# Softmax sums on 64 partitions by columns of ones beside V, reciprocals in pieces, single K and V buffers

## The reference

```python
Q = (x @ Wq + bq) * scale ; K = (x @ Wk + bk) * scale ; V = x @ Wv + bv
Qr = transpose(Q.reshape(B*H, 64, L)) ; Kr = K.reshape(B*H, 64, L)
w = softmax(Qr @ Kr)                       # 8192 x 8192 for each of 32 heads
x = layernorm(x + (w @ Vr).reshape(B, L, D) @ Wo + bo)
gamma = mean(abs(W)) ; Wq1 = clip(round(W1 / (gamma + 1e-5)), -1, 1)   # W2 alike
x = layernorm(x + relu(x @ Wq1.T + b1) @ Wq2.T + b2)
```

## Time and profile before

| | |
|---|---|
| median of 3 runs | 2467.16 us (2321.94 to 2620.44) |
| profiled execution | 2328.56 us |
| its span, slowest core (6) | 2326.9 us; cores 2295.7 to 2326.9 |
| granted TensorE clock | 0.972 on core 6, 0.972 to 0.978 over the cores |
| TensorE busy | 2127.2 us, 91% |
| ScalarE busy | 1936.2 us, 83% |
| VectorE busy | 605.4 us, 26% |
| GpSimd busy | 185.1 us, 8% |

### The profile page before, as it was taken

One profiled execution on the slowest core, in us unless ns is written; L12 is line 12 of the kernel. 1 busy time (PEld: TensorE's weight loads), 2 busy tenths in 40 slices (PEclk: granted clock), 3 DMA queues, 4 the chain that ended last, 5 costly groups with the idle time before them and its releaser, 6 DMA issues.

```text
span 2326.9 us, 48854 instructions; the slowest of 8 cores (2295.7 to 2326.9 us)
## 1 busy us (share of the span) xinstructions
PE 2127.2 (91%) x17698; PEld 1108.4 (48%) x17712; DVE 605.4 (26%) x796; ACT 1936.2 (83%) x2050; POOL 185.1 (8%) x253
## 2 busy tenths in 40 slices
PE   2999859999988999999999999999999999999498
PEld 0455435455444455555454555555455555554143
DVE  0334223344446441111122111011131111011332
ACT  0589759899988899999999999999999999999000
POOL 0000020000012000001111000010120000011200
PEclk8999879999999999999999999999999999999799
DMA  9556454556656541224302111243211112343147
GB/s 171 124 138 140 106 150 124 116 151 168 164 163 183 169 137 52 74 92 137 114 18 80 47 56 56 92 133 96 73 29 56 47 51 69 101 131 112 29 155 256
DMA packets 95811, 253.33 MB, mean 109 GB/s; under 512 B 29792, under 2 KB 30048, under 8 KB 94048
## 3 DMA queue, kind: packets, MB, share of 16 engines
q1 hardware_dynamic: 86496, 220.45, 32.3%
q0 software_dynamic: 9088, 29.76, 5.9%
HBM read 224.71 MB, written 33.85 MB: 111 GB/s over the span
## 4 chain that ended last, share of the span: by engine, by line
PE 60%; ACT 13%; DMA 12%; issue 6%; DVE 5%; another core or an unknown queue 2%; POOL 1%; ACTq 0%; DVEq 0%; SPq 0%; POOLq 0%
PE psO L749 25%; PE psF L652 16%; ACT PT L782 13%; PE psS L722 10%; PE psS L697 4%; PE psS L724 4%; DMA rec_bc<-rec 3%; DMA den<-den 2%; PE psF L697 2%; DMA rec<-rec 1%; DMA Wch<-W 1%; DMA x<-x 1%; DMA den<-o_sb 1%; DVE A L933 1%
## 5 line engine op out<-in xcount | busy, mean ns | idle before, releaser
L782 ACT ACTIVATE PT<-psS 128x1024 bf16<-128x1024 f32 x2048 | 1934.8, 1034 | 214.3 <-PE psS L724 198.3
L749 PE MATMUL psO<-PT,V 64*65 64x512 bf16 x8192 | 1328.9, 378 | 0.6 <-ACT PT L782 0.2
L722 PE MATMUL psS<-Q,K 64*128 64x512 bf16 x2048 | 770.9, 376 | 38.2 <-ACT PT L782 15.1
L724 PE MATMUL psS<-Q,K 64*128 64x512 bf16 x2048 | 779.3, 381 | 0.0
L749 PEld LDWEIGHTS psO<-PT,V 64*65 64x65 bf16 x8192 | 560.8, 108 | 339.9 <-issue 119.7
L722 PEld LDWEIGHTS psS<-Q,K 64*128 64x128 bf16 x2048 | 190.8, 93 | 439.0 <-issue 381.4
L652 PE MATMUL psF<-x1T,ring 64*128 64x512 bf16 x1536 | 311.6, 379 | 12.5 <-DVE hT L834 11.7
L652 PE MATMUL psF<-ring,hT 64*128 64x512 bf16 x1536 | 280.8, 377 | 4.0 <-DVE x L841 2.8
L724 PEld LDWEIGHTS psS<-Q,K 64*128 64x128 bf16 x2048 | 190.6, 93 | 34.3 <-issue 3.2
L834 DVE TENSOR_SCALAR hT<-psF,b1c 128x512 bf16<-128x512 f32 x106 | 74.7, 747 | 334.5 <-PE psF L652 324.1
L933 DVE TENSOR_TENSOR A<-o_sb,rec_bc 64x512 bf16<-64x512 f32 x64 | 66.4, 1037 | 281.6 <-DMA rec_bc<-rec 280.6
(11 more groups left out here) (74 smaller groups left out, 769.9 us busy)
## 6 DMA issues: line engine op xcount, KB each, us to landing
ring<-wq SPq DMA_DIRECT2D x192, 512.0 KB, 3.8
Wch<-W SPq DMA_DIRECT2D x128, 512.0 KB, 5.1
wq<-qout SPq DMA_DIRECT2D x64, 256.0 KB, 5.6
Q<-qs SPq DMA_DIRECT2D x64, 128.0 KB, 4.6
rec_bc<-rec POOLq DMA_DIRECT2D x32, 256.0 KB, 4.0
x<-x POOLq DMA_DIRECT2D x16, 512.0 KB, 8.6
y<-x SPq DMA_DIRECT2D x16, 512.0 KB, 2.9
xT<-xT POOLq DMA_DIRECT2D x4, 1024.0 KB, 36.3
```

Of the source, the lines that this page charges most:

```text
L722: e.matmul(psS[:, at:at + 512], K[h % 2][0:64, g * 128:g * 128 + 128], Q[0:64, q:q + 512], start=True, stop=True, tile_position=(0, 0))
L724: e.matmul(psS[:, at + 512:at + 1024], K[h % 2][64:128, g * 128:g * 128 + 128], Q[64:128, q:q + 512], start=True, stop=True, tile_position ...
L749: return e.matmul(psO[0:65, half * 512:half * 512 + 512], V[h % 2][lo:lo + 64, v:v + 65], PT[lo:lo + 64, at:at + 512], start=(g == 0 and s ...
L782: e.activation(PT[:, (s % PTR) * 1024:(s % PTR) * 1024 + 1024], psS[:, (s % 2) * 1024:(s % 2) * 1024 + 1024], AF.Exp, scale=SOFT_SCALE).th ...
```

## The change

- V's tile gets 128 columns, 64 of V and 64 of ones, so rows 64 to 127 of `psO` all hold the sums. `o_sb` is 128x1024. `denominators`, `reciprocals`, their four DMAs, `den` and `rec_bc` go.
- `invert` becomes eight reciprocals of 64x128 from `o_sb`'s rows 64 to 127 into `rec`, `divide` two halves as before. `side_plan()` gives these ten items and the preparation's chunks each a step of its own that is not next to an eviction.
- The preparation goes on every fourth step where that is free (before: fourth, and sixth for the quantised ones), with longer gaps around the block's start, and has three `Wch` buffers. W1's last chunk is at step 568, W2's at 785; the first f1 group is at 602, the first f2 at 806.
- One K and one V. All of heads 1 to 3 go through `stg` and DRAM and are loaded in quarters during the last block of the head before, each when its quarter has been used. V's quarter is two DMAs of 128x8 rows of 128 bytes.
- `O_AT` is 25. An o group waits for the two blocks that it reads.
- The loads of bo and b2 stand behind the first scores, on their own semaphore, which GpSimd waits for.

VectorE's list around the start of the second block, before: copies of `psO`, evictions of K of head 1, chunks (`gcol<-Wch`), and the sums' items.

```diff
-REC_AT, MUL_AT, O_AT = 11, 19, 21
+CR = 3 ; O_AT = 25 ; RECS = 8 ; KV_AT = 22
+def side_plan():
+    ...
+    def is_free(s, long):
+        return not (s in norm or s in ends or s - 1 in ends or s + 1 in ends or long and s + 2 in ends
+                    or s % STEPS in (1, 2, 3) or long and s % STEPS == 0)
+
+    for p in range(NB * NP - 1):
+        s = STEPS * (p + 1) + 4
+        for k in range(RECS + 2):
+            while not is_free(s, False):
+                s += 1
+            norm[s] = (p, k)
+            s += 1
+    s = 6
+    for i in range(128):
+        if i in (32, 64):
+            s += 14
+        while not is_free(s, i >= 64) or i >= 64 and s + 1 in norm:
+            s += 1
+        prep[s] = i
+        s += 4
...
-STAGED = [g for g in PRO + ATT if g[0] == "q" or (g[0] == "k" and g[1] >= 2)]
+STAGED = [g for g in PRO + ATT if g[0] == "q" or (g[0] in "kv" and g[1] >= 1)]
...
-    o_sb = alloc("o_sb", [65, 1024], F32)
-    rec_bc = alloc("rec_bc", [64, 1024], F32)
+    o_sb = alloc("o_sb", [128, 1024], F32)
+    rec = alloc("rec", [64, 1024], F32)
...
+            def load_kv(h, m):
+                p = NP * h - 1
...
+                e.wait_ge(pS, STEPS * p + 16 * m + 16)
+                e.dma_start(K[:, m * 1024:m * 1024 + 1024],
+                            AP(ksh, h * 524288 + m * 1024, [[4096, 128], [1, 1024]])).then_inc(sK[m], 16)
+                e.wait_ge(pV, value_count(p, 8 * m + 7))
+                for j in (2 * m, 2 * m + 1):
+                    e.dma_start(AP(V, j * 1024, [[8192, 128], [128, 8], [1, 64]]),
+                                AP(vsh, h * 524288 + j * 64, [[4096, 128], [512, 8], [1, 64]])).then_inc(sV[m], 16)
...
-                if kind == "o" and i == 0:
-                    e.wait_ge(sW["o"], 16)
-                    e.wait_ge(vMul, 2 * NP * (h + 1))
+                if kind == "o":
+                    if i == 0:
+                        e.wait_ge(sW["o"], 16)
+                    e.wait_ge(vMul, 2 * (NP * h + 2 * i + 2))
...
+                if p % NP == 0 and h >= 1 and r % 16 == 0:
+                    e.wait_ge(sK[r // 16], 16 * h)
...
+                if p % NP == 0 and h >= 1 and fb == 0:
+                    e.wait_ge(sV[m], 32 * h)
...
-                    return e.matmul(psO[0:65, half * 512:half * 512 + 512], V[h % 2][lo:lo + 64, v:v + 65],
+                    return e.matmul(psO[:, half * 512:half * 512 + 512], V[lo:lo + 64, v:v + 128],
...
+            e.memset(AP(V, 64, [[8192, 128], [128, 64], [1, 64]]), 1.0)
...
+            def invert(p, k):
+                if k == 0:
+                    e.wait_ge(vO, p + 1)
+                c = k * (1024 // RECS)
+                e.reciprocal(rec[:, c:c + 1024 // RECS], o_sb[64:128, c:c + 1024 // RECS]).then_inc(vRec, 1)
...
-            e.wait_ge(sBias, 6 * 16)
+            e.wait_ge(sBias, 4 * 16)
...
+                if s in NORM:
+                    normalize_queries(*NORM[s])
```

More of the change, by code:

```diff
@@ L24 @@
 WR = 6
+CR = 3
+O_AT = 25
 SOFT_SCALE = float(2.0 ** -10)
@@ L128, in bank @@
     return i % 3, (G - 3 if i >= 3 else G - 1 if i == 0 else -1)
[L132 to L136, removed]
+def side_plan():
+    ends = set(ENDS)
+    norm, prep = {}, {}
+    def is_free(s, long):
[9 more added lines that the diff above has]
+    s = 6
     for i in range(128):
         if i in (32, 64):
-            s += 12
-        while s in busy or s % STEPS in (1, 2, 3, 4, REC_AT, MUL_AT):
+            s += 14
+        while not is_free(s, i >= 64) or i >= 64 and s + 1 in norm:
             s += 1
[L142 to L153, removed]
+        prep[s] = i
+        s += 4
+    return norm, prep
+NORM, PREP = side_plan()
+NORMED = {p: s for s, (p, k) in NORM.items() if k == RECS + 1}
+assert all(NORMED[NP * h - 1] < HSTEPS * h + O_AT for h in range(1, NB))
+THR_AT = {s: i // 32 for s, i in PREP.items() if i in (31, 63)}
 QUANT_END = [next(s for s, i in PREP.items() if i == n) for n in (95, 127)]
@@ L185 @@
 SR = 3
+KV_AT = 22
 def build_nc():
@@ L520, in _ @@
             e.wait_ge(pS, 1)
-            prep_load(0)
-            prep_load(1)
+            e.dma_start(bo_bc[:, :], AP(boh, 0, [[0, 128], [1, 1024]])).then_inc(sBias2, 16)
+            e.dma_start(b2_bc[:, :], AP(b2h, 0, [[0, 128], [1, 1024]])).then_inc(sBias2, 16)
+            for i in range(CR):
+                prep_load(i)
             chunk = 0
@@ L746, in one @@
                     lo = 64 * upper
-                    v = (fb * 8 + 2 * m + odd) * 65
+                    v = ((2 * m + odd) * 8 + fb) * 128
                     at = ((2 * g + half) % PTR) * 1024 + odd * 512
-                    return e.matmul(psO[0:65, half * 512:half * 512 + 512], V[h % 2][lo:lo + 64, v:v + 65],
-                                    PT[lo:lo + 64, at:at + 512], start=(g == 0 and side == 0 and odd == 0),
+                    return e.matmul(psO[:, half * 512:half * 512 + 512],
+                                    V[lo:lo + 64, v:v + 128], PT[lo:lo + 64, at:at + 512], start=(g == 0 and side == 0 and odd == 0),
                                     stop=(g == 31 and side == 1 and odd == 1), tile_position=(lo, 0))
@@ L796, in _ @@
             e.memset(warm[0:1, 0:8], 0.0).then_inc(vInit, 1)
-            for i in range(2):
-                e.memset(AP(V[i], 64, [[4160, 128], [65, 64], [1, 1]]), 1.0)
-            e.memset(vstg[:, :], 1.0)
+            e.memset(AP(V, 64, [[8192, 128], [128, 64], [1, 64]]), 1.0)
             def evacuate(G):
@@ L948, in _ @@
                     take_sums(p)
-                if r == REC_AT and p >= 0:
-                    invert(p)
-                if r == MUL_AT and p >= 0:
-                    divide(p)
+                if s in NORM:
+                    normalize_queries(*NORM[s])
                 if s in PREP:
@@ L960, in _ @@
             take_sums(p)
-            invert(p)
-            divide(p)
+            for k in range(RECS + 2):
+                normalize_queries(p, k)
             for G in range(NATT, len(GROUPS)):
```

166 lines of the change are left out of this document (59 added, 107 removed).

## The result

The changed kernel takes 0.975 of the time before, 95% interval 0.971 to 0.979: 2262.56 us against 2320.18 us, the lowest of four runs each.

A forecast was written before the change was run, and what follows sets the result against it. ScalarE and TensorE were taken as full at 0.965 us a step, with some 94 us lost in attention stalls. 2328.6 - 62.5 (trip) - 14 (prologue) - 10.7 (tail) + 5 (burst) + 5 (preparation, reciprocals) = 2251.4 us; range 2215 to 2305.

The forecast's parts named there:

- the burst: Stretch at 317 us: Wo and four tiles of x still load at once there, so 5 us of its loss was left.
- how the numbers follow: Closing odds: within 2225 to 2282 us 0.70; faster by over 2% 0.75, within 2% 0.16, slower 0.09.
- a lower clock: Rival: 64 more columns of ones lower TensorE's granted clock; gain gone at 0.96, 2471 us at 0.9; chance 0.06.
- the term of the preparation: W1 and W2 chunks at four-step spacing: store waits mostly hidden, 5 us allowed together with the reciprocals.
- The trip, -62.5 us: Attention: removing the sums' four DMAs through DRAM, and the waits for them, was to save 62.5 us.
- six stretches: Disturbed stretches at 242, 317, 660, 742, 800 and 1490 us, laid to the sums' trip, losing 62.5 us together.
- Reciprocals: VectorE, each query block: eight 64x128 pieces of 850 ns plus divides take 8.9 us, fitting ten steps of 9.65 us.
- 128 columns: 0: Value matmuls: weight loads 15 ns shorter if anything, beside matmuls, so 0 us; bounds 0 and 40 us gain.
- K and V: Single buffers loaded by quarters: V's at most 17.8 us a quarter, landing before need, so 0 us.
- Prologue and tail: Start: first exponential at 70.6 us, -14 us; end: output groups run during the reciprocals, -10.7 us.
- Crowding by reciprocals: Rival: VectorE's longer reciprocals delay an eviction each block; 1.2 us pieces give 2318 us; chance 0.09 no change, 0.03 slower.
- The wait only changes its DMA: Rival: VectorE still waits for chunk loads and stores, half of the 62.5 us returns, 2283 us; chance 0.07.

## Why the prediction was right or wrong

**The number.** 2251 us was made for executions like the profiled one; those take 2262.56 and 2263.92 us, 11 and 13 more, and the direction and the 2% were right. In the attention the forecast left 18.5 us in the stretches (8.5 for the preparation, 5 for the burst, 5 for stores and reciprocals) and 34.2 are there; 4.6 us less are lost outside of them, which I had not counted, and that part is luck. The median of all four runs, 2344.91, lies outside 2215 to 2305. The step that failed there is how the numbers follow: I gave a lower clock 0.06 and held it for something that the change might bring, though two of the three runs shown of before lay 6% and 13% above the lowest. A range for the median had to reach up by as much. Of the mechanism, the step that failed is the term of the preparation, below.

**The trip, -62.5 us.** Right in kind: no such wait is left. Mis-sized: alone it is 51.6 us in the attention. I took the whole of six stretches for it, and behind it stood waits for chunks and for the threshold that it had hidden. The 5 us that I left for the burst are about half of the 11 us that are missing.

**The preparation, 5 us together with the reciprocals.** This step failed most. The stretches of the preparation went from 8.5 to 34.2 us. I had worked out that a store buffer comes back after 8.2 us against 7.7 us for eight steps, and took the difference for some tenths of a us that the room between evictions would hide. Two things were wrong. The 8.2 us were built on the median landing of 5.6 us: in front of the stall at 604 us the stores took 8.62, 6.99 and 7.22 us to land, and a buffer came back after 8.2 to 11.9 us, 10 on average. And the lateness doesn't end with each pair of chunks: it adds up over a row of them (7.5 us over eight, the rows above), until the next eviction or copy of sums pays for it. In all VectorE waited 68.1 us for stores, and ScalarE stood for 8.21, 3.90 and 6.92 us at 604, 653 and 710 us. Four buffers take 20 us off. The forecast set the chunks' six-step spacing against four steps and did not ask what six steps had hidden. The threshold I left as it was; its 24 us against 11 steps show as soon as VectorE is not late for another reason, and are worth 8 us.

**Reciprocals.** 153 + 128 x 5.4 = 850 ns; measured 903 ns, 830 in a row (6.63 / 8):

```profile
L732 PEld LDWEIGHTS psO<-PT,V 64*128 64x128 bf16 x8192 | 499.9, 94 | 379.3 <-issue 138.1
...
L903 DVE RECIPROCAL rec<-o_sb 64x128 f32<-64x128 f32 x256 | 215.5, 903 | 4.5
...
L909 DVE TENSOR_TENSOR A<-o_sb,rec 64x512 bf16<-64x512 f32 x64 | 73.0, 1141 | 4.0
L879 DVE TENSOR_SCALAR tq<-Wch,thr 128x1024 bf16<-128x1024 f32 x64 | 48.1, 751 | 70.7 <-DMA wq<-qout 68.1 <-DVE qout L880 1.8 <-DVE mv L829 0.6
```

The divides rose from 1.04 to 1.14 us. The 64x1024 form gives (6548 - 903) / 896 = 6.3 ns an element, against my 5.4. The Trainium skill ("VectorE: DVE Perf Modes", walkthrough of the 8-slice pipeline) says that a reciprocal repeats its divide eight times; worked out from that, as an estimate, an element takes 8.3 ns and a piece 1.07 us and a fixed part, and the trace, with 6.3 ns and 0.90 us, doesn't agree. The price of crowding, however, was wrong as a rule: doubled reciprocals should have cost 5.8 us a block and cost 2.2. By the plan the evictions stand at different places of the row (steps 12, 11 and 9 of the first three blocks, and none near it in the eighth), and I take it that only what is in front of an eviction counts; no run shows that by itself.

**128 columns: 0.** Right within what can be told. The row of after is 94 ns, as for every load of 128 columns. The rule of a time that grows with columns (the Trainium skill, "TensorE: Matmul & The Clock Gate", LDWEIGHTS) gives 54 ns for 65 columns, as an estimate, and does not fit the 108 ns that they take.

**K and V.** V's quarters are hidden:

```profile
V<-vs SPq DMA_DIRECT2D x24, 128.0 KB, 5.1
```

5.1 us for 1024 rows of 128 bytes; my upper bound was 8.9. No first score or value matmul waits for K or V.

**Prologue and tail.** -13.4 against -14 and -10.6 against -10.7, each by its own rows; alone in the kernel before the prologue's part is 10.2 us. One cost I did not see: `O_AT` at 25 brings a group's end next to a block's. In three places TensorE waits for the copy because of it, 3.6 of the 10.6 us in the table of waits (the other 7.0 are the late stores'), and `O_AT` at 21 takes them back.

**The rivals.** Crowding by reciprocals is real at twice their size; at the true size it doesn't show in the undisturbed stretch, with 544 steps in 525 us as before. "The wait only changes its DMA" came true for some 26 us (34.2 less 8.5) of the 31 that it named; the time still lies 20 us under its 2283, since 10 of them were allowed for in the sum and 4.6 were won elsewhere. A lower clock from more columns doesn't show in the undisturbed stretch, and the kernel before, with 65 columns, had a lower clock too in a run beside the first experiments (0.91 on one die, 2433.23 us).

## What to carry to other kernels

When a late DMA in front of an in-order engine is taken out, list what else that engine was waiting for at the same time, for these waits come forward. A ring of two buffers whose turn-round (work, store to landing, issue) comes within 10% of its period by median times deserves a price of its own: here two more buffers took 20 us off, because the stores landed later than the median just where they were needed, and the lateness added up from chunk to chunk. A long instruction on an engine that also evicts PSUM is best cut into pieces that the evictions can pass between: with the same 6.6 us of reciprocals in one piece, and the plan that followed from it, the kernel took 75 to 80 us more.

## What the runs showed of the hardware

A VectorE reciprocal of fp32 took 240 ns for 16 elements a partition, 903 ns for 128 and 6548 ns for 1024, 6.3 ns an element between the last two. A weight load of 65 columns took 108 ns and one of 128 took 93 to 94 ns, beside the same matmuls. The threshold's two dependent DMAs took 24 us together both times in the changed kernel, the first of them, 128 rows of 4 bytes, 10.36 and 17.99 us. A DMA of 1024 rows of 128 bytes landed in 5.1 us (median of 24). Stores of the same 256 KB landed after 4.4 to 9.1 us between 540 and 720 us of the changed kernel.
